# Four graph layers on one core: narrow sort one-hots in place of wide ones, destinations loaded first, and four pieces of work in other places

## What is computed

```
summed = segment_sum(x[src], dst); deg = segment_sum(1, dst)
neighbor_mean = summed / max(deg, 1)
out = relu(einsum('of,nf->no', w, concat([x, neighbor_mean])))
```

## Time and profile before

| | before |
|---|---|
| runs | 1571.47, 1567.6, 1570.6 us (median 1570.6) |
| profiled execution | 1571.28 us, its span 1569.8 us |
| TensorE busy | 1370.8 us, 87% |
| TensorE weight load busy | 884.0 us, 56% |
| VectorE busy | 1353.6 us, 86% |
| ScalarE busy | 903.3 us, 58% |
| GpSimd busy | 479.7 us, 31% |
| mean granted TensorE clock | 0.949 |

### The profile page before, as it was taken

How to read it: one execution, slowest core, us unless ns; L and a number is a source line. 1 busy time by engine, 2 the same in 40 slices (tenths; PEclk the granted TensorE clock), 3 DMA queues, 4 the chain that set the end, 5 groups by cost and what they waited for, 6 DMA issues and landing times.

```text
span 1569.8 us, 25159 instructions
## 1 busy us (share of the span) xinstructions
PE 1370.8 (87%) x8237; PEld 884.0 (56%) x8237; DVE 1353.6 (86%) x2066; ACT 903.3 (58%) x1949; POOL 479.7 (31%) x488
## 2 busy tenths in 40 slices
PE   2877988738688878689999999978999999999998
PEld 1555444512333333476666666765667777776465
DVE  7965999999899999869999999887989989997244
ACT  1176555718555555568888888642258849772400
POOL 1688888840001101226666666200000000000000
PEclk9799999859699999789999999988999999999999
DMA  8001000026211121247666766500144435333401
GB/s 195 4 6 8 7 7 7 6 79 173 69 56 57 37 72 22 69 131 214 204 197 191 216 201 195 91 1 1 41 147 135 134 121 174 135 134 100 126 20 46
DMA packets 77815, 150.27 MB, mean 96 GB/s; under 512 B 14850, under 2 KB 33396, under 8 KB 77605
## 3 DMA queue, kind: packets, MB, share of 16 engines
q1 hardware_dynamic: 51395, 83.19, 16.5%
q0 software_dynamic: 23328, 59.50, 14.9%
q10 hardware_dynamic: 3010, 6.59, 1.5%
HBM read 116.13 MB, written 32.91 MB: 95 GB/s over the span
## 4 chain that ended last, share of the span: by engine, by line
PE 45%; DVE 29%; issue 16%; ACT 5%; DVEq 3%; DMA 1%; POOL 0%; SPq 0%; POOLq 0%; ACTq 0%
PE PS L1320 14%; DVE arena L2084 7%; DVE arena L2050 5%; PE PS L1272 4%; DVE arena L2246 4%; PE PS L1330 4%; DVE arena L2080 3%; PE PS L1405 3%; PE PS L942 3%; ACT arena L1468 2%; PE PS L1385 2%; PE PS L1395 2%; DVEq L2246 2%; DVE arena L2005 2%; PE PS L1301 1%
## 5 line engine op out<-in xcount | busy, mean ns | idle before, releaser
L728 POOL DMA_INDIRECT recs<-arena x170 | 238.6, 1404 | 90.9 <-issue 90.3
L1090 PE MATMUL PS<-arena 125*128 125x512 f32 (+1 forms) x480 | 190.5, 535 | 41.6 <-DVE arena L2084 41.6
L792 POOL DMA_INDIRECT arena<-xup,gidx x205 | 195.0, 951 | 101.4 <-issue 49.3
L1178 PEld LDWEIGHTS PS<-arena 128*32 128x32 f32 x3280 | 173.1, 109 | 86.4 <-ACT arena L1706 79.8
L1706 ACT ACTIVATE arena<-arena,gslot 128x32 f32<-128x32 f32 x820 | 186.2, 309 | 51.8 <-PE PS L1178 45.4
L1178 PE MATMUL PS<-arena 128*32 128x128 f32 (+1 forms) x3280 | 200.4, 304 | 4.7 <-DVE arena L2238 2.2
L2238 DVE TENSOR_TENSOR arena<-PS,arena 128x1536 f32<-128x1536 f32 (+1 forms) x103 | 179.3, 1740 | 0.0
L1090 PEld LDWEIGHTS PS<-arena 125*128 125x128 f32 x480 | 86.0, 191 | 146.2 <-issue 78.1
L1638 ACT ACTIVATE arena<-arena,c 125x1250 f32<-125x1250 f32 x80 | 106.7, 1336 | 97.3 <-DVE arena L2080 97.2
L1320 PE MATMUL PS<-arena,cnt_d 128*125 128x256 f32 x576 | 147.8, 379 | 0.0
L2080 DVE SCALAR_TENSOR_TENSOR arena<-arena,c 125x1250 f32<-125x1250 f32 (+1 forms) x100 | 138.1, 1384 | 11.0 <-ACT arena L1760 9.9
(11 more groups left out here) (395 smaller groups left out, 2537.6 us busy)
## 6 DMA issues: line engine op xcount, KB each, us to landing
arena<-in_spline_wT SPq DMA_DIRECT2D x32, 512.0 KB, 4.0
t_rows<-arena SPq DMA_DIRECT2D x18, 512.0 KB, 5.0
arena<-t_rows SPq DMA_DIRECT2D x18, 512.0 KB, 4.5
arena<-uv_rows SPq DMA_DIRECT2D x14, 610.4 KB
arena<-h_rows SPq DMA_DIRECT2D x26, 256.0 KB
h_rows<-arena SPq DMA_DIRECT2D x24, 256.0 KB, 2.8
arena<-xup,gidx POOLq DMA_INDIRECT x205, 3.6
cnt_rows<-cnt_s SPq DMA_DIRECT2D x1, 2734.4 KB
```

Of the source, the lines that this page charges most:

```text
L728: pool.indirect_dma_start(out=recs, out_offset=bass.IndirectOffsetOnAxis(pos[:, c:c + 1], 0), in_=rec[:, c, :], in_offset=None).then_inc(s ...
L792: pool.indirect_dma_start(out=ring[:, m, :], out_offset=None, in_=xup, in_offset=bass.IndirectOffsetOnAxis(gidx[:, par, m:m + 1], 0))\
L1090: ins = t.matmul(PS[:, 3 * par + q, 0:n1 - n0], hs[:, sblk, par * C:par * C + 2 * C], wt[:, sblk % WR, n0:n1], start=(sblk == 0), stop=(sb ...
L1178: ins = t.matmul(PS[quad * DB:(quad + 1) * DB, bank, o0 * MUL:o0 * MUL + w], sel4[:, s, v * DB:(v + 1) * DB], prod[:, s, c0 * MUL:c1 * MUL ...
```

## The change

- **Sort one-hots.** The wide instructions go, and `scale_lanes` on ScalarE with them. VectorE makes each column by three tensor_scalar instructions whose scalars are one f32 per partition: `lane_src` and `lane_dl` (is_equal to the lane, times the source or destination number; 128 elements, two scalars) and `tile_oh` (is_equal to the tile; 204 elements, one scalar). The buffers are no longer laid out in pairs. VectorE's five memsets of `cnt_d` become five ScalarE copies of 2504 zeros behind the first round (`clear_counts`).
- **Destinations first.** All other opening loads of SP and of ScalarE's queue wait until the destinations have landed.
- **xup** gets seven staging buffers in place of two.
- **rec_rows** does ten transposes to 128 partitions in place of ten products to 64.
- **Degrees.** `degrees(0)` stands behind `half_terms(1)`.
- **Passage rows.** `index_big` stands behind four `z_low`, in place of ahead of the first.
- **Own part of layer 3.** ScalarE copies each own part from PSUM to `self_sb` (four buffers), and `add4` takes two VectorE operations in place of three.

```diff
-        tile_f, lane_f = dstf.bitcast(f16)[:, 0:EC], posf.bitcast(f16)[:, 0:EC]
-        src_f = dstf.bitcast(f16)[:, EC:2 * EC]
+        lane_f, tile_f, src_f = (at(off, [NP, EC]) for off in (10240, 10410, 10580))
...
-        xup_st = at(19500, [NP, 2, D])
+        xup_st = tuple(at(o, [NP, D]) for o in (10240, 10752, 11264, 11776, 12288, 19500, 20012))
...
+        self_sb = at(16848, [NP, 4, D])
...
+            for r in ROWS:
+                sp.dma_start(dsti[r], a["dst"].rearrange("(p e) -> p e", p=NP)[r]).then_inc(s_dst_in, 16)
+            sp.wait_ge(s_dst_in, 32)
             for dst_tile, view, done in (
-                    (dsti, a["dst"].rearrange("(p e) -> p e", p=NP), s_dst_in),
...
             def sort_batch(j):
                 pe.wait_ge(s_sort_ok, j + 1)
-                pe.wait_ge(s_lane_cp, j + 1)
...
                 for b in range(NB):
-                    ins = t.matmul(PS[C:2 * C, b // 4, (b % 4) * NP:(b % 4 + 1) * NP],
-                                   rcol[:, 1, b:b + 1].to_broadcast([NP, C]), ident[:NP, :NP], start=True, stop=True,
-                                   tile_position=(0, C))
+                    ins = t.transpose(PS[:, b // 4, (b % 4) * NP:(b % 4 + 1) * NP], rcol[:, 1, b:b + 1].to_broadcast([NP, 128]),
+                                      ident[:NP, :NP])
...
             def self_part(b):
                 if b >= len(SB4):
-                    pe.wait_ge(s_y3_cp, b - len(SB4) + 1)
+                    pe.wait_ge(s_self_cp, b - len(SB4) + 1)
...
+            act.wait_ge(s_dst_in, 32)
             for r in ROWS:
                 act.dma_start(x_sb[r, 0:HB, :], a["x"].rearrange("(b p) n -> p b n", p=NP)[r, 0:HB, :]).then_inc(s_x_in, 16)
...
-            for j in range(ROUNDS):
-                scale_lanes(j)
-                if j in (4, 9):
-                    gat_out(NB - 2 + j // 9)
...
+            act.wait_ge(s_sort_ok, 1)
+            act.wait_ge(s_consts, 1)
+            for j in range(NB // 2):
+                ins = clear_counts(j)
+            ins.then_inc(s_const0, 1)
+            for b in range(NB - 2, NB):
+                gat_out(b)
+            for q in range(3):
+                quad_out(q, 2 + q % 2)
+            for q in range(2):
+                rows_out(q)
...
+            for b in range(3):
+                self_in(b)
             act.wait_ge(s_bigrow_in, 32)
             A(big_z[:], big_zrow, ACT.Copy).then_inc(s_z_cp, 1)
+            self_in(3)
             for b in range(NB):
                 ln_sqrt(4, b)
+                if b + 4 < NB:
+                    self_in(b + 4)
...
-                v.tensor_tensor(lane_oh[:, rs], numbers(128), of_pairs(lane_f, 128), ALU.is_equal).then_inc(s_lane_ok, 1)
-                v.tensor_tensor(tile_oh[:, rs], numbers(NSORT), of_pairs(tile_f, NSORT), ALU.is_equal)
-                dve.wait_ge(s_lane_ok, j + 1)
-                v.tensor_tensor(lane_src[:, rs], lane_oh[:, rs], of_pairs(src_f, 128), ALU.mult).then_inc(s_sort_ok, 1)
-                if 4 <= j < 9:
-                    ins = v.memset(cnt_d[:, (j - 4) * 2 * SPAN:(j - 3) * 2 * SPAN], 0)
...
+                for n in range(SB):
+                    r, c = (j % SBUFS) * SB + n, j * SB + n
+                    lane, tile = lane_f[:, c:c + 1], tile_f[:, c:c + 1]
+                    v.tensor_scalar(lane_src[:, r, :], iota_src[:NP, 0:128], lane, src_f[:, c:c + 1], ALU.is_equal, ALU.mult)
+                    v.tensor_scalar(lane_dl[:, r, :], iota_src[:NP, 0:128], lane, dl1[:, c:c + 1], ALU.is_equal, ALU.mult)
+                    ins = v.tensor_scalar(tile_oh[:, r, :], iota_src[:NP, 0:NSORT], tile, None, ALU.is_equal)
+                ins.then_inc(s_sort_ok, 1)
...
-            degrees(0)
             half_tiles(0)
             half_terms(1)
+            degrees(0)
...
-            index_big()
             for b in range(NB):
+                if b == len(ZB) - 1:
+                    index_big()
...
-                link(v.tensor_scalar(fin[:, b % 2, :], PS[:NP, 3 * (b % 2), :], deg[:, b:b + 1], None, ALU.mult))
-                link(v.tensor_tensor(fin[:, b % 2, :], fin[:, b % 2, :], PS[:NP, SB4[b % len(SB4)], :], ALU.add))
+                dve.wait_ge(s_self_cp, b + 1)
+                link(v.scalar_tensor_tensor(fin[:, b % 2, :], PS[:NP, 3 * (b % 2), :], deg[:, b:b + 1], self_sb[:, b % 4, :],
+                                            ALU.mult, ALU.add))
```

More of the change, by code:

```diff
@@ L230, in build @@
         iota2 = sb("iota2", [128, 2 * NT], f16)
[L231 to L234, removed]
+        lane_src, lane_dl = (at(off, [NP, SBUFS * SB, 128], f16) for off in (1020, 2940))
+        tile_oh = cnt_s[:].rearrange("p b n -> p (b n)")[:, 4 * N:4 * N + SBUFS * SB * NSORT].bitcast(f16)\
+            .rearrange("p (a c) -> p a c", a=SBUFS * SB)
         srt_s, srt_d = sb("srt_s", [128, NSORT]), sb("srt_d", [128, NSORT], f16)
@@ L455, in build @@
         s_zrow_out = sem("s_zrow_out")
+        s_self_ps = sem("s_self_ps")
+        s_self_cp = sem("s_self_cp")
         s_bigrow_in = sem("s_bigrow_in")
@@ L625, in _ @@
                 for r in ROWS:
-                    sp.dma_start(xup[b * NP:(b + 1) * NP, :][r], xup_st[r, b % 2, :])\
-                      .then_inc(s_xup_out0 if b % 2 == 0 else s_xup_out1, 16)
+                    sp.dma_start(xup[b * NP:(b + 1) * NP, :][r], xup_st[b % len(xup_st)][r])\
+                      .then_inc(s_xup_out0 if b < NB - len(xup_st) else s_xup_out1, 16)
             with sp.Fori(0, G // 4 - 1) as i:
@@ L834, in sort_batch @@
                 pe.wait_ge(s_sort_ok, j + 1)
[L835 removed]
                 for n in range(SB):
[L837 removed]
+                    r = (j % SBUFS) * SB + n
                     for q, lane in enumerate((lane_src, lane_dl)):
[L839 removed]
+                        ins = t.matmul(PS[:, q, 0:NSORT], lane[:, r, :], tile_oh[:, r, :],
                                        start=(j == 0 and n == 0), stop=(j == ROUNDS - 1 and n == SB - 1))
@@ L1392, in self_part @@
                 if b >= len(SB4):
-                    pe.wait_ge(s_y3_cp, b - len(SB4) + 1)
+                    pe.wait_ge(s_self_cp, b - len(SB4) + 1)
                 for k in range(KT):
-                    t.matmul(PS[:NP, SB4[b % len(SB4)], :], xT3[:, k, b * NP:(b + 1) * NP], w_self[:, k, :],
-                             start=(k == 0), stop=(k == KT - 1))
+                    ins = t.matmul(PS[:NP, SB4[b % len(SB4)], :], xT3[:, k, b * NP:(b + 1) * NP], w_self[:, k, :],
+                                   start=(k == 0), stop=(k == KT - 1))
+                ins.then_inc(s_self_ps, 1)
             def near_part(b):
@@ L1460, in evac_uv, with clear_counts @@
                 ins.then_inc(ok, 1)
[L1462 to L1469, removed]
+            def clear_counts(j):
+                return A(cnt_d[:, j * 2 * SPAN:(j + 1) * 2 * SPAN], ones[:NP, 0:1].to_broadcast([NP, 2 * SPAN]), ACT.Copy, scale=0.0)
             def gat_out(b):
@@ L1672, in xup_out @@
                 act.wait_ge(s_xup_ps, b + 1)
-                if b >= 2:
-                    act.wait_ge(s_xup_out0 if b % 2 == 0 else s_xup_out1, 32 * (b // 2))
-                A(xup_st[:, b % 2, :], PS[:NP, 2 + b % 2, :], ACT.Copy, scale=float(MUL) ** -0.5).then_inc(s_xup_cp, 1)
+                if b >= len(xup_st):
+                    act.wait_ge(s_xup_out0, 32 * (NB - len(xup_st)))
+                A(xup_st[b % len(xup_st)], PS[:NP, 2 + b % 2, :], ACT.Copy, scale=float(MUL) ** -0.5).then_inc(s_xup_cp, 1)
                 if b == 3:
```

27 lines of the change are left out of this document (7 added, 20 removed).

## The result

The changed kernel takes 1613.1 us (median of four runs, 1610.3 to 1615.4), the kernel before 1569.1 (four runs): a ratio of 1.028, 95% interval 1.026 to 1.030. It is 44 us slower; 27 were forecast. In the profiled executions the span went from 1569.8 to 1611.1 us, +41.3.

| start of | before, us | after, us | shift |
|---|---|---|---|
| first sort one-hot | 70.39 | 68.34 | -2.05 |
| copy of the sorted lists | 146.72 | 199.04 | +52.3 |
| maxima of layer 0's scores | 286.0 | 336.1 | +50.1 |
| products after the maxima | 402.3 | 453.9 | +51.6 |
| layer 0's last reciprocals | 646.8 | 698.5 | +51.7 |

The account below looks back on a forecast made before the run. It took the chain of waits between TensorE and VectorE, in the sort stage through ScalarE's 170 scalings, as the bound. Sort stage +29.4, meetings +8.5, other edits -10.6 gave +27.3 us: 1598 us, range 1560 to 1635 (forecast's own 1587 to 1612).

Parts of the forecast that it names:

- meetings with the scatters: Sort stage: VectorE's one-hots lose time beside GpSimd's scatters, 0.28 us at each of 62; 0 to 17 us, taken as 8.5.
- destinations: Opening: destinations loaded ahead of all else let VectorE start 3.9 us earlier (bounds 0 and 6.04).
- column price: Sort stage: three narrow VectorE instructions cost 0.62 us a column of edges, 105.4 us for 170 columns.
- behind the stage: After the sort stage: the other edits on the chain together gain 10.6 us.
- Rivals 1 and 2: Sort one-hots: both scalars hidden, 0.34 us a column, 1542 us (18%); or second scalar free, 0.50, 1576 us (10%).
- The sign that the copy starts between 174 and 190: End of the sort stage: the copy to srt_s starting between 174 and 190 us would show the forecast right.
- rec_rows: Ten transposes instead of ten plain products on TensorE gain 1.7 us (bounds 0 and 2).
- degrees: Layer 2's attention: the degree reduction moves into VectorE's wait before the second half, gaining 3.95 us.
- passage: Passage rows of layer 3: TensorE's stop at block 5 goes, 1.65 us, and 1.8 more comes back without a stop.
- last layer: Layer 3: ScalarE copies each self part, VectorE needs two operations rather than three; gain 0.7 us at the last block.
- xup: Before layer 1's first gather: seven staging buffers spare ScalarE a wait for a store, gaining 0.8 us.
- Rival 3, starved scatters: Sort stage: scatters find no gap beside the one-hots, so the edge network ends late; 1627 to 1662 us, 10%.

Follow-up runs that it names:

- e3: The changed kernel with the second scalar of the two 128-wide one-hots as a number in the instruction; 1584.1 us in one run, copy of the sorted lists at 169.62.
- e2: The changed kernel with numbers in the instruction in place of all per-partition scalars of the one-hots; 1564.0 us in one run, copy of the sorted lists at 139.62.
- e4: The changed kernel with only the first 20 of 170 record scatters; copy of the sorted lists 16.8 us sooner; its whole time, 1619.7 us, isn't compared.
- e6: e5 with GpSimd's index rows put behind its masks and held until VectorE has made its 40 comparisons of destinations; 1568.4 us, ratio 1.000 to the kernel before.
- e7: e6 with two staging buffers for xup again rather than seven; 1566.9 us, ratio 0.999 to the kernel before.
- e5: The changed kernel with four wide VectorE one-hot instructions a sort round and no ScalarE scalings; 1571.7 us, ratio 1.002 to the kernel before.
- e11: e6 with the diagonal additions and two copies moved from behind sort round 10 to ahead of round 3; 1541.9 us, ratio 0.9825 to the kernel before.
- e8: e6 with one wait of VectorE for its own last instruction at the end of each sort round; 1544.6 us, ratio 0.985 to the kernel before.
- e10: e6 with the four diagonal additions and two copies moved from behind sort round 10 to behind the last round; 1556.5 us, ratio 0.992 to the kernel before.

## Why the prediction was right, and where its size was off

The direction and the mechanism held; the sum was 14 us short on the profiled execution (+27.3 against +41.3). The median of 1613.1 lies in the stated range (1560 to 1635) and 1 us above the forecast's own (1587 to 1612). Of the 14 us the meetings with the scatters are 10.0, the destinations 1.9, the column price 1.7 and a term that I left out 0.9; behind the stage 0.4 came back.

- **Column price.** 0.62 forecast, 0.63 measured, so 170 x 0.63 = 107.1 against 105.4. Building it from one instruction with one scalar and one with two, each start to start, was right to 2%. The step from f32 to 16-bit elements in it (twice the cost) is not shown by any run on its own; the 0.06 that e3 gives for the second scalar is. Rivals 1 and 2 (hidden scalars, second one free) are out by e2 and e3. The Trainium skill's price by elements alone ("VectorE: DVE Perf Modes", the TRN2 errata) fits e2's instructions without scalars (an estimated (58 + 32)/0.96 = 94 ns, measured 100) and misses the form used (220): the scalars are missing in it.
- **Meetings with the scatters: the mis-sized term.** I took 8.5 us, at most 17. From 68.34 to 194.88 VectorE worked 126.54 us; less 107.1 and 0.94 for the small work of round 10 (which I hadn't summed), 18.5 are left, for 85 scatters 0.22 each; e4 took 16.8 off. What failed is the step from 17 to 8.5: I halved the result for want of a reason, and every scatter met VectorE. The 17 itself was near by luck, since two errors in it offset each other: 0.28 at a meeting (0.22 measured), and 62 meetings from the mean pace of all scatters (1.70 us), although a scatter that is never held up takes 1.48, and 85 fell into the longer stage. The sign that the copy starts between 174 and 190 failed with it (199.04).
- **Destinations first.** Forecast -3.9, measured -2.05. They landed sooner than I thought (VectorE starts at 3.16, 5.3 earlier), and 3.2 us went at once: 1.0 in L1864 and 2.2 in the 40 comparisons, beside GpSimd's index rows (e6). That VectorE would be moved into another engine's work was not in the sum.
- **Behind the stage.** Forecast -10.6, measured -11.0 from the copy to the end. rec_rows 2.1 (1.7 forecast), degrees 3.8 (3.95), passage 3.5 (3.45, with no stop at block 5 and the block at 3.68 us), last layer 0.7 (0.7). xup's 0.8 is not seen (e7), and layer 1's loop lost 1.8 between its first and its last product, nearly all of it in the 32 slow products. Between the copy and the maxima 2.2 us were won and between the maxima and the products after them 1.5 lost; I haven't looked into these. So four terms came out as forecast, and that the sums agree to 0.4 us is luck: the shifts that I had not foreseen nearly cancel.
- **Rival 3, starved scatters,** did not happen in the changed kernel: its last scatter started at 318.7, 17.5 us sooner than before. VectorE was the one that waited. It did happen in e2, e3 and e5 to e7. The sum that I made for it (what the edge network's lateness costs beyond its slack) is what decided e5. One figure in it was wrong: by its rows the lateness that costs nothing was 38 us (431.7 less 393.4), not 42.

## What to carry to other kernels

Price a narrow VectorE instruction by its scalars per partition: two of them more than double a 128-wide 16-bit one (0.10 to 0.22 us), so the 30 narrow ones of a round (6.3 us) lose to 4 wide ones (3.35). Beside indirect DMAs of GpSimd, look at the longest one and the last one's start, not at the median: a faster VectorE stage (e5) can be a slower kernel. Small unrelated instructions go where the engine waits anyway.

## What the runs showed of the hardware

- The meeting of VectorE and GpSimd can go either way. In the changed kernel each scatter runs its 1.18 us and VectorE loses 0.22; in e5 one scatter hangs for 20.65 us through six rounds of wide instructions, after some two dozen had passed, most at 1.17 or 1.56; in the opening a 0.28 us instruction takes 1.27 beside an index row of 1.18.
- The Trainium skill ("SBUF — State Buffer", Who interferes with whom) has the later one wait until the earlier instruction ends, and names tensor_scalar in a two-port mode and, beside a GpSimd instruction that reads SBUF, a VectorE instruction with two SBUF inputs. The opening agrees (the 1.27 us instruction ends at 4.60, 0.11 after the index row), and so does the scatter beside the scan in e11 (it ends at 53.87, 0.99 after the scan). The sort rounds agree in part: the one-hot that is held ends with the scatter, but those ahead of it passed during the same scatter, so that 0.22 us are lost and not 1.18; and the 20.65 us are not one VectorE instruction but about two dozen.
- In all six kernels with an odd scatter in the sort stage (e2, e3, e5 to e8) it began beside the four additions and two copies or less than 0.5 us behind them; moving those away ended it (e10, e11), and one wait a round shortened it to 4.08 us (e8). In the changed kernel the scatter that met them (149.96, the additions from 149.62) took 1.19. What makes a scatter miss its turn stays open.
